# Head 0's row maxima in one part or in two: the start of attention in a two-block graph and attention kernel

## The chip, the cores and the metric

One core of a Trainium2 chip runs the whole program. The metric is device time in microseconds (us), the median of three runs. Before the change it is 898.85 us (897.73 to 899.95).

## The reference

Four blocks act on a matrix `x` of 1354 rows by 256 columns, each with a residual: a graph product with an adjacency matrix, an attention block with a mixture of experts, a graph attention block, and a second mixture of experts. The change touches the attention alone. Cut to what matters it is, with 8 heads of width 32:

```
h = layernorm(x)*g + b
q = h@wq + bq;  k = h@wk + bk;  v = h@wv + bv      # 1354 x 256, 8 heads of 32
scores = q_h @ k_h.T / sqrt(32)                    # 1354 x 1354 per head
attn = softmax(scores, axis=-1)                    # every row minus its own maximum
ctx = attn @ v_h
x = x + ctx @ wo + bo
```

## The kernel before, in words

The 1354 rows are padded to 11 tiles of 128. Every engine has its own instruction list in program order and waits on semaphores: TensorE (PE) multiplies, VectorE (DVE), ScalarE (ACT) and GpSimd (POOL) do elementwise work, SyncE (SP) issues most DMAs. `q` and `k` are each written to memory as a high and a low part, then loaded as "stacks" for one head (`load_stack`, L605): `q_st` and `k_st` have 96 rows of head width (high, high, low against high, low, high), and two more rows in which `q_st` carries the negated row maxima and `k_st` carries ones. So one product gives scores with the maximum already taken off.

**Projections.** `q` and `k` are made in 16 pieces (`qk_product`, L1179). The last 8 belong to heads 4 to 7 and are made while head 0 is already being worked on. For each of these 8, ACT makes two copies (`qk_high`, L897, lines L903 and L904), POOL subtracts (L758), and SP stores the high and the low part (`store_qk`, L589, lines L593 and L595). Three buffers rotate. ACT does not start the first exponential until all stores have landed (L932), because the exponentials' buffers lie over the projections' buffers.

**Maxima.** Row maxima are found in "slots". A slot (`fill_slot`, L1201, on PE; `empty_slot`, L1727, on DVE) is one product of 128 query rows by 452 keys (L1212) and one `tensor_reduce` that takes the maximum of each row (L1736). Three such chunks cover a row tile, 33 a head. The slots share three PSUM banks, so slot i waits until slot i-3 is emptied. When a head's 33 chunks are done, three small DVE instructions make the negated maxima as a high and a low part (`neg_max`, L1740, lines L1743, L1745 and L1747). Later a special slot, the "turn" (list `TURN`, L541), transposes them on PE (L1207), DVE copies them to `m_rows` (L1733), and SP loads that into the two extra rows of `q_st` (`load_max`, L616, line L618). SP issues it for head 0 behind the stores of the projections and ahead of the third stack.

**Scores and values.** With maxima in place, PE computes the scores of a head transposed, in units of 128 keys by 452 queries (`scores`, L1216, line L1224); three thirds of the queries by 11 key tiles make 33 units a head. ACT takes the exponential of each (`exps`, line L915), and PE multiplies it with the values (`values`, L1228, line L1232; two records a unit in the trace, because the operands are full fp32). The units go in groups of 4, 4 and 3 (`GROUPS`). The order on PE is written out by hand (L1263 to L1282): in "phase" j PE alternates a slot and a score unit of group j+1, then fills what slots are left of those allotted to the phase, then does the values of group j. A third's values leave PSUM once per 3 phases (`copy_third`).

**How the slots are spread.** `BESIDE` = 4 slots follow each of the 8 late projection pieces, slots 32 to 41 stand alone (`FILL` = 42), then four score units of group 0, then phase 0 begins. `slots_by(phase)` (L552) gives phases 0 to 13 these numbers of slots: 5, 5, 5, 5, 4, 5, 5, 5, 4, 5, 5, 5, 5, 4. From phase 14 on it is 3 or 4 each. The turns are slots 35, 71, 105 and so on. There are 272 slots, and the last is in phase 56 of 0 to 71. Beside all this POOL splits the weights of the last block (L786 to L796) into high and low parts, from the end of its last subtraction for the projections.

Of the kernel before, what the change touches and what calls it, by code (L numbers as in the profile page):

```python
# [15 lines left out]
P = 128  # L16
# [99 lines left out]
def build_program(nc, a, out):  # L116
    with ExitStack() as ctx:
# [422 lines left out]

        TURN = [(h + 1) * CHUNKS + h + min(4 if h else 2, (H - 1 - h) * CHUNKS) for h in range(H)]  # L541
        SLOTS = H * CHUNKS + H

# [3 lines left out]

        FILL = TURN[0] + 7
        BESIDE = 4
        AHEAD = 14  # L550

        def slots_by(phase):  # L552

            return min(SLOTS, FILL + -(-SLOTS * (phase + 1) // len(GROUPS)) + min(phase + 1, AHEAD))

# [3 lines left out]
        def _(sp):  # L559
# [55 lines left out]

            def load_max(h):  # L616
                sp.wait_ge(s_mx, TURN[h] + 1)
                sp.dma_start(q_st[h % 3].bitcast(F32)[3 * DK:3 * DK + 2, :].rearrange("c (t p) -> c t p", p=P),  # L618
                             m_rows.bitcast(F32)[:, :]).then_inc(s_mload[h % 3], 16)

# [5 lines left out]
            for n in range(HALF, 2 * HALF):  # L626
                store_qk(n)
            load_max(0)
            load_stack(2)
# [12 lines left out]
            for h in range(H):  # L642
                if h >= 1:
                    if h + 2 < H:
                        if h + 2 == H // 2:
                            stored(2 * HALF)
                        sp.wait_ge(s_s2, h * UNITS)
                        load_stack(h + 2)
                    store_third(h - 1, 2)
                    if h + 1 < H:  # L650
                        load_values((h + 1) % 2, h + 1)
                store_third(h, 0)
                if h + 1 < H:
                    load_max(h + 1)
                if h + 1 < H:
                    store_third(h, 1)
# [452 lines left out]
        def _(pe):  # L1109
# [91 lines left out]
            def fill_slot(i):  # L1201
# [3 lines left out]
                if i in TURN:  # L1205
                    pe.wait_ge(s_hl, TURN.index(i) + 1)
                    pe.transpose(ps[0:2 * T, i % 3, 0:P], m_hl.bitcast(F32)[:, :], ident).then_inc(s_s1, 1)  # L1207
                else:
# [7 lines left out]
            def scores(g):  # L1216

                h, m = divmod(g, UNITS)
                third, kt = divmod(m, T)
                if m == 0:  # L1220
                    pe.wait_ge(s_mload[h % 3], h // 3 * 16 + 16)
                if g >= 3:
# [377 lines left out]
        def _(dve):  # L1600
# [126 lines left out]
            def empty_slot(i):  # L1727
                dve.wait_ge(s_s1, i + 1)
                if i in TURN:
                    h = TURN.index(i)  # L1730
                    if h >= 1:
                        dve.wait_ge(s_mload[(h - 1) % 3], (h - 1) // 3 * 16 + 16)
                    dve.tensor_copy(m_rows[:, :], ps[0:2 * T, i % 3, 0:P]).then_inc(s_mx, 1)  # L1733
                else:
                    h, n = chunk_of(i)
                    dve.tensor_reduce(mx4[:, n // KB, n % KB:n % KB + 1], ps[:, i % 3, 0:KC], AX_X, ALU.max).then_inc(s_mx, 1)  # L1736
                    if n == CHUNKS - 1:
                        neg_max(h, i)

            def neg_max(h, i):  # L1740

                dve.wait_ge(s_mx, i + 1)
                dve.tensor_reduce(negm[:, :], mx4[:, :, :], AX_X, ALU.max).then_inc(s_mq, 1)  # L1743
                dve.wait_ge(s_mq, h * 2 + 1)
                dve.tensor_scalar(m_hl[:, 0:T], negm[:, :], -1.0, None, ALU.mult).then_inc(s_mq, 1)  # L1745
                dve.wait_ge(s_mq, h * 2 + 2)
                dve.scalar_tensor_tensor(out=m_hl[:, T:2 * T], in0=negm[:, :], scalar=-1.0, in1=m_hl.bitcast(F32)[:, 0:T],  # L1747
                                         op0=ALU.mult, op1=ALU.subtract).then_inc(s_hl, 1)

# [496 lines left out]
```

## Time and profile before

| | |
|---|---|
| median of three runs | 898.85 us (897.73 to 899.95) |
| profiled execution, own time | 897.19 us |
| its span | 895.4 us |
| granted TensorE clock, mean over the span | 0.928 |
| late projection pieces with slots beside | 98.06 to about 118.5 us |
| first score unit of head 0 | 124.92 us |
| first exponential of head 0 | 125.73 us |
| phases 0 to 13 | 126.87 to 181.11 us |
| last slot | 322 us |
| last value product of head 7 | 367 us |

The profile is one execution. Its span runs from its first to its last instruction, and its own time has 1.8 us more around it. A timeline row gives the start, the length, the engine, the line, what is written and read, and how many instructions were merged; in brackets stands how long the engine sat idle before and what released it. PE instructions overlap, so a start tells more than a length. The PE clock has two levels, 1.0 (2.4 GHz) and 0.5 (1.2 GHz); a value between them is a mean over a stretch that has both.

### The profile page before, as it was taken

The numbers are of one execution on the slowest core, as the hardware profiler recorded it, in microseconds if no ns is written. First come the engines' busy times: TensorE is split into PE (matmuls) and PEld (weight loads), VectorE is DVE, ScalarE is ACT, GpSimd is POOL, SyncE is SP. The second block draws the span as 40 slices with busy tenths as digits, with TensorE's granted clock in tenths as the row PEclk, the third lists the DMA queues.
The fourth block names the chain that finished last, engine by engine and source line by source line (L and its number), as shares of the span: only waits on it lengthen the run. The fifth ranks groups of instructions, "written<-read, shape, count | busy, mean of one in ns | idle before, by whom it ended". The sixth has DMA issues, their size and how long they took to land. (4 is left out here: it accounts for less than half of the span.)

```text
span 895.4 us, 13738 instructions
## 1 busy us (share of the span) xinstructions
PE 781.5 (87%) x4218; PEld 588.8 (66%) x4219; DVE 602.7 (67%) x1164; ACT 410.8 (46%) x840; POOL 315.6 (35%) x322
## 2 busy tenths in 40 slices
PE   3897999999999999843999974999768999999993
PEld 3895655555555543533999972687746888888882
DVE  6575677766666687774989865697593656665661
ACT  3224434556655656351666732631332444445441
POOL 2100246667665766714433004000011343334422
PEclk9998979999999999975999996999758999999997
DMA  7537766887787667633345305950652387752210
GB/s 268 191 95 283 197 205 224 253 264 252 253 267 243 232 200 232 219 112 132 131 147 212 120 26 190 388 187 15 279 182 80 50 269 228 229 154 36 32 17 0
DMA packets 60782, 158.86 MB, mean 177 GB/s; under 512 B 20796, under 2 KB 39034, under 8 KB 57788
## 3 DMA queue, kind: packets, MB, share of 16 engines
q1 hardware_dynamic: 39788, 97.85, 32.2%
q0 software_dynamic: 20944, 60.38, 21.9%
q8 instruction: 27, 0.44, 0.2%
q14 instruction: 23, 0.19, 0.1%
HBM read 103.00 MB, written 49.93 MB: 171 GB/s over the span
## 5 line engine op out<-in xcount | busy, mean ns | idle before, releaser
L1736 DVE TENSOR_REDUCE mx<-ps 128x1 f32<-128x452 f32 x264 | 148.1, 621 | 65.7 <-PE ps L1212 64.8
L915 ACT ACTIVATE expo<-ps 128x452 f32<-128x452 f32 x264 | 124.3, 551 | 92.6 <-PE ps L1224 91.5
L1092 ACT ACTIVATE h<-ps,b_l 128x128 f32<-128x128 f32 x232 | 63.2, 384 | 123.7 <-PE ps L1555 120.2
L1232 PE MATMUL ps<-expo,v_st 128*64 128x452 f32 (+1 forms) x576 | 117.3, 529 | 0.0
L1212 PE MATMUL ps<-k_st,q_st 96*128 96x452 f32 x264 | 106.6, 417 | 4.7 <-DVE mx L1736 4.4
L1224 PE MATMUL ps<-q_st,k_st 98*128 98x452 f32 x264 | 97.1, 392 | 2.0 <-ACT expo L915 2.0
L852 POOL DMA_INDIRECT out<-y1t,out_row x29 | 46.2, 1592 | 124.5 <-DVE share L2129 97.3
L2147 DVE COPY h1pre<-ps 128x1024 f32<-128x1024 f32 x29 | 35.5, 1225 | 78.5 <-PE ps L1548 78.5
L1568 PE MATMUL ps<-w_ring,h_hi 128*128 x232 | 84.2, 400 | 2.8 <-DVE y1t L2156 2.8
L1212 PEld LDWEIGHTS ps<-k_st,q_st 96*128 96x128 f32 x264 | 51.0, 193 | 51.7 <-DVE mx L1736 34.8
L792 POOL TENSOR_TENSOR part_lo<-part,part_hi 128x512 fp32r<-128x512 f32 x64 | 80.9, 1289 | 0.5
L835 POOL DMA_INDIRECT x1t<-x_d,goal x29 | 29.8, 1028 | 135.8 <-DVE goal L2103 115.3
L1232 PEld LDWEIGHTS ps<-expo,v_st 128*64 128x64 f32 x576 | 35.4, 137 | 54.3 <-issue 46.5
L1570 PE MATMUL ps<-w_ring,h_lo 128*128 x232 | 65.7, 283 | 0.0
L1224 PEld LDWEIGHTS ps<-q_st,k_st 98*128 98x128 f32 x264 | 50.3, 195 | 17.8 <-ACT expo L915 9.2
L806 POOL DMA_INDIRECT xs<-x_d,goal x24 | 33.1, 1380 | 69.4 <-PE ps L1350 36.9
L786 POOL CAST part_hi<-part 128x1024 fp32r<-128x1024 f32 x32 | 36.0, 1124 | 55.8 <-DMA part<-w_l 55.8
L1568 PEld LDWEIGHTS ps<-w_ring,h_hi 128*128 128x128 f32 x232 | 44.2, 191 | 13.8 <-issue 3.3
L1546 PE MATMUL ps<-w_ring,x_hi 128*128 x116 | 49.6, 428 | 3.9 <-issue 3.8
L1134 PE MATMUL ps<-hid_hi,adj_hi 128*128 128x256 f32 x121 | 33.0, 303 | 17.6 <-ACT adj_hi L887 17.6
L981 ACT ACTIVATE h<-ps,b_l 128x272 f32<-128x272 f32 x64 | 31.1, 486 | 35.6 <-issue 20.1
L1548 PE MATMUL ps<-w_ring,x_lo 128*128 x116 | 46.7, 403 | 0.0
(322 smaller groups left out, 1792.9 us busy)
## 6 DMA issues: line engine op xcount, KB each, us to landing
w_l<-w_l SPq DMA_DIRECT2D x8, 2053.0 KB, 8.4
part<-w_l POOLq DMA_DIRECT2D x32, 512.0 KB, 5.4
w_split_d<-part_hi POOLq DMA_DIRECT2D x32, 512.0 KB, 3.5
w_split_d<-part_lo POOLq DMA_DIRECT2D x32, 512.0 KB, 3.9
adj<-adj_t SPq DMA_DIRECT2D x22, 704.0 KB, 5.0
w_ring<-w_split_d SPq DMA_DIRECT2D x8, 1365.5 KB
w_ring<-w_split_d SPq DMA_DIRECT2D x4, 1365.0 KB
q_st<-q_hi_d SPq DMA_DIRECT2D x16, 176.0 KB, 3.8
```

Of the source, the lines that this page charges most:

```text
L792: last = pool.tensor_tensor(part_lo[k][:, half], part[k][:, half], part_hi.bitcast(F32)[:, half], ALU.subtract)
L852: pool.indirect_dma_start(out=out[:, :], out_offset=bass.IndirectOffsetOnAxis(ap=out_row[:, t:t + 1], axis=0), in_=y1t[t % 2][:, :], in_of ...
L915: act.activation(expo[g % 8][:, :], ps[:, 3 + g % 3, 0:QC], ACT.Exp, scale=SCALE).then_inc(s_exp, 1)
L1092: last = act.activation(h1[:, f, :], ps[:, 4 + f // 4, (f % 4) * P:(f % 4 + 1) * P], ACT.Gelu_apprx_tanh, bias=b1_l1[:, bass.ds(e, 1), f])
L1212: pe.matmul(ps[:, i % 3, 0:KC], q_st[h % 3][0:3 * DK, (n // KB) * P:(n // KB + 1) * P], k_st[h % 3][0:3 * DK, (n % KB) * KC:(n % KB + 1) * ...
L1224: pe.matmul(ps[:, 3 + g % 3, 0:QC], k_st[h % 3][0:3 * DK + 2, kt * P:(kt + 1) * P], q_st[h % 3][0:3 * DK + 2, third * QC:(third + 1) * QC] ...
L1232: return pe.matmul(ps[at:at + 2 * DK, 6 + g // T % 2, lo:hi], v_st[h % 2][:, kt, :], expo[g % 8][:, lo:hi], start=kt < 2, stop=kt == T - 1 ...
L1546: pe.matmul(ps[:, 2 + b, :], x1_hi[:, kt, :], part_of(at), start=kt == 0, stop=False)
L1548: mm = pe.matmul(ps[:, 2 + b, :], x1_lo[:, kt, :], part_of(at), start=False, stop=kt == DT - 1)
L1568: pe.matmul(ps[:, 6, :], h1_hi[k][:, f, :], part_of(at, 2 * D), start=f == 0, stop=False, skip_group_check=True)
L1570: mm = pe.matmul(ps[:, 6, 0:D], h1_lo[k][:, f, :], part_of(at, D), start=False, stop=f == FT - 1, skip_group_check=True)
L1736: dve.tensor_reduce(mx4[:, n // KB, n % KB:n % KB + 1], ps[:, i % 3, 0:KC], AX_X, ALU.max).then_inc(s_mx, 1)
```

## The change

Head 0's maxima get two turns. The first (slot 14) comes when row tiles 0 to 3 have their maxima, which cover the 452 queries of the first third; the second (slot 36) carries tiles 4 to 10. The first score units of head 0 wait only for the first load, those of the second third wait for the second load. Three slots follow each late projection piece, none stands alone ahead of the scores (`FILL` = 24), and the phases get 7, 7, 7, 7, 6, 7, 7, 7, 7, 6, 6, 4, 4, 4 slots up to phase 13, after which the count is that of before with the one turn more. The other heads keep one turn each, one to two slots later in number. SP issues the first load after the store of the fifth late piece and the second where the only one stood.

```diff
-        TURN = [(h + 1) * CHUNKS + h + min(4 if h else 2, (H - 1 - h) * CHUNKS) for h in range(H)]
-        SLOTS = H * CHUNKS + H
+        EARLY = -(-QC // P)
+        TURN = [EARLY * KB + 2] + [(h + 1) * CHUNKS + h + 1 + min(4 if h else 2, (H - 1 - h) * CHUNKS) for h in range(H)]
+        TURNED = [(0, 0, EARLY), (0, EARLY, T)] + [(h, 0, T) for h in range(1, H)]
+        SLOTS = H * CHUNKS + len(TURN)
...
-        FILL = TURN[0] + 7
-        BESIDE = 4
-        AHEAD = 14
+        def maxima_landed(h):
+            return h // 3 * 16 + (32 if h % 3 == 0 else 16)
+
+        BESIDE = 3
+        FILL = BESIDE * HALF
+        AHEAD = 32
+        CATCH_UP = 3
 
         def slots_by(phase):
 
-            return min(SLOTS, FILL + -(-SLOTS * (phase + 1) // len(GROUPS)) + min(phase + 1, AHEAD))
+            return min(SLOTS, FILL + -(-SLOTS * (phase + 1) // len(GROUPS)) + min(CATCH_UP * (phase + 1), AHEAD))
...
-            def load_max(h):
-                sp.wait_ge(s_mx, TURN[h] + 1)
-                sp.dma_start(q_st[h % 3].bitcast(F32)[3 * DK:3 * DK + 2, :].rearrange("c (t p) -> c t p", p=P),
-                             m_rows.bitcast(F32)[:, :]).then_inc(s_mload[h % 3], 16)
+            def load_max(n):
+                h, lo, hi = TURNED[n]
+                sp.wait_ge(s_mx, TURN[n] + 1)
+                sp.dma_start(q_st[h % 3].bitcast(F32)[3 * DK:3 * DK + 2, lo * P:hi * P].rearrange("c (t p) -> c t p", p=P),
+                             m_rows.bitcast(F32)[0:2 * (hi - lo), :]).then_inc(s_mload[h % 3], 16)
...
             for n in range(HALF, 2 * HALF):
                 store_qk(n)
-            load_max(0)
+                if (n - HALF + 1) * BESIDE == TURN[0] + 1:
+                    load_max(0)
+            load_max(1)
             load_stack(2)
...
                 if h + 1 < H:
-                    load_max(h + 1)
+                    load_max(h + 2)
...
                 if i in TURN:
                     pe.wait_ge(s_hl, TURN.index(i) + 1)
-                    pe.transpose(ps[0:2 * T, i % 3, 0:P], m_hl.bitcast(F32)[:, :], ident).then_inc(s_s1, 1)
+                    h, lo, hi = TURNED[TURN.index(i)]
+                    pe.transpose(ps[0:2 * (hi - lo), i % 3, 0:P], m_hl.bitcast(F32)[:, 2 * lo:2 * hi], ident).then_inc(s_s1, 1)
...
-                if m == 0:
-                    pe.wait_ge(s_mload[h % 3], h // 3 * 16 + 16)
+                if g == 0:
+                    pe.wait_ge(s_mload[0], 16)
+                elif m == (T if h == 0 else 0):
+                    pe.wait_ge(s_mload[h % 3], maxima_landed(h))
...
-                    dve.tensor_copy(m_rows[:, :], ps[0:2 * T, i % 3, 0:P]).then_inc(s_mx, 1)
+                    turn = TURN.index(i)
+                    h, lo, hi = TURNED[turn]
+                    if turn == 1:
+                        dve.wait_ge(s_mload[0], 16)
+                    elif turn:
+                        dve.wait_ge(s_mload[(h - 1) % 3], maxima_landed(h - 1))
+                    dve.tensor_copy(m_rows[0:2 * (hi - lo), :], ps[0:2 * (hi - lo), i % 3, 0:P]).then_inc(s_mx, 1)
...
+                    if (h, 0, n // KB + 1) in TURNED[:1] and n % KB == KB - 1:
+                        neg_max(0, i)
                     if n == CHUNKS - 1:
-                        neg_max(h, i)
-
-            def neg_max(h, i):
-
+                        neg_max(h + 1, i)
+
+            def neg_max(turn, i):
+
+                _, lo, hi = TURNED[turn]
                 dve.wait_ge(s_mx, i + 1)
-                dve.tensor_reduce(negm[:, :], mx4[:, :, :], AX_X, ALU.max).then_inc(s_mq, 1)
+                dve.tensor_reduce(negm[:, lo:hi], mx4[:, lo:hi, :], AX_X, ALU.max).then_inc(s_mq, 1)
...
```

The two other instructions of `neg_max` are cut to the same tiles in the same way.

## Rows read from the trace of the kernel before

**Rows 1.** The page's costliest group: busy, mean ns, idle before it.
```profile
L1736 DVE TENSOR_REDUCE mx<-ps 128x1 f32<-128x452 f32 x264 | 148.1, 621 | 65.7 <-PE ps L1212 64.8
```
**Rows 2.** Timeline of PE, late projections to first scores: start, length, instruction, idle before.
```profile
99.08 1.05 PE L1212 MATMUL ps<-k_st,q_st 96*128 96x452 f32 x3
100.44 0.47 PE L1212 MATMUL ps<-k_st,q_st 96*128 96x452 f32 x1 [0.31 <-DVE mx L1736]
100.75 1.35 PE L1185 MATMUL ps<-nt,w_attn 128*128 128x352 f32 x4
...
116.26 1.35 PE L1185 MATMUL ps<-nt,w_attn 128*128 128x352 f32 x4
...
124.92 2.15 PE L1224 MATMUL ps<-q_st,k_st 98*128 98x452 f32 x4
```
**Rows 3.** Timeline of DVE, head 0's negated maxima.
```profile
120.65 0.19 DVE L1743 TENSOR_REDUCE negm<-mx 128x11 f32<-128x33 f32 x1
...
121.17 1.16 DVE L1736 TENSOR_REDUCE mx<-ps 128x1 f32<-128x452 f32 x2
...
122.24 0.27 DVE L1733 CAST m_rows<-ps 22x128 fp32r<-22x128 f32 x1
```
**Rows 4.** Timeline of all engines: last projection piece from copy to store, first exponential.
```profile
117.64 0.51 ACT L903 ACTIVATE proj<-ps,vecs 128x298 f32<-128x298 f32 x1 [1.59 <-PE ps L1185]
...
119.02 0.93 POOL L758 TENSOR_TENSOR proj_lo<-proj,proj_hi 128x352 fp32r<-128x352 f32 x1 [1.96 <-ACT proj_hi L904]
...
119.98 0.32 SPq L595 DMA_DIRECT2D k_lo_d<-proj_lo  x1
...
125.73 1.93 ACT L915 ACTIVATE expo<-ps 128x452 f32<-128x452 f32 x4 [6.79 <-PE ps L1224]
```
**Rows 5.** DMA issues by tensor: KB each, median us from issue to landing.
```profile
k_lo_d<-proj_lo SPq DMA_DIRECT2D x8, 176.0 KB, 1.8
```
**Rows 6.** Stretches by engine: us, busy (count) of PE, PEld, DVE, ACT, POOL; PE clock; DMA.
```profile
121.00:122.00 1.00, 0.53 (x2) 0.25 (x2) 0.97 (x4) 0.00 (x0) 0.00 (x0) 0.67 0.90 184
131.00:132.00 1.00, 1.00 (x6) 0.38 (x4) 0.13 (x1) 0.00 (x0) 0.00 (x0) 0.71 0.99 397
```
**Rows 7.** The same columns for phases 0 to 13 together, 1, 4, 5 and 12.
```profile
126.87:181.11 54.24, 52.28 (x231) 28.73 (x229) 39.11 (x73) 27.11 (x57) 35.31 (x39) 0.96 0.76 244
132.63:136.42 3.79, 3.77 (x18) 1.91 (x16) 2.77 (x5) 1.43 (x3) 3.48 (x5) 1.00 0.47 156
143.64:146.96 3.32, 3.32 (x17) 1.73 (x16) 2.23 (x4) 1.42 (x3) 2.44 (x3) 1.00 0.89 263
146.96:151.89 4.93, 3.62 (x19) 2.08 (x17) 4.17 (x8) 1.86 (x4) 3.24 (x4) 1.00 0.52 188
173.40:178.00 4.60, 4.01 (x19) 2.10 (x17) 3.47 (x8) 2.41 (x5) 3.62 (x5) 1.00 0.71 247
```
**Rows 8.** Timeline of PE inside phases 0 and 3.
```profile
130.39 2.31 PE L1232 MATMUL ps<-expo,v_st 128*64 128x452 f32 x8
...
139.84 0.47 PE L1212 MATMUL ps<-k_st,q_st 96*128 96x452 f32 x1
...
141.64 0.40 PE L1212 MATMUL ps<-k_st,q_st 96*128 96x452 f32 x1
141.97 1.74 PE L1232 MATMUL ps<-expo,v_st 128*64 128x452 f32 x8
```
**Rows 9.** Timeline of all engines in phase 5, with head 1's negated maxima.
```profile
147.47 0.63 DVE L1736 TENSOR_REDUCE mx<-ps 128x1 f32<-128x452 f32 x1 [1.09 <-PE ps L1212]
...
148.34 1.03 POOL L786 CAST part_hi<-part 128x1024 fp32r<-128x1024 f32 x1 [1.96 <-DMA part<-w_l]
...
148.36 1.04 DVE L1745 TENSOR_SCALAR m_hl<-negm 128x11 fp32r<-128x11 f32 x1
...
149.52 2.23 DVE L1736 TENSOR_REDUCE mx<-ps 128x1 f32<-128x452 f32 x4
150.20 0.19 PEld L1212 LDWEIGHTS ps<-k_st,q_st 96*128 96x128 f32 x1 [1.70 <-DVE mx L1736]
```

More of the change, by code:

```diff
@@ L1729, in empty_slot @@
                 if i in TURN:
-                    h = TURN.index(i)
-                    if h >= 1:
-                        dve.wait_ge(s_mload[(h - 1) % 3], (h - 1) // 3 * 16 + 16)
-                    dve.tensor_copy(m_rows[:, :], ps[0:2 * T, i % 3, 0:P]).then_inc(s_mx, 1)
+                    turn = TURN.index(i)
[5 more added lines that the diff above has]
+                    dve.tensor_copy(m_rows[0:2 * (hi - lo), :], ps[0:2 * (hi - lo), i % 3, 0:P]).then_inc(s_mx, 1)
                 else:
@@ L1736, in empty_slot @@
                     dve.tensor_reduce(mx4[:, n // KB, n % KB:n % KB + 1], ps[:, i % 3, 0:KC], AX_X, ALU.max).then_inc(s_mx, 1)
+                    if (h, 0, n // KB + 1) in TURNED[:1] and n % KB == KB - 1:
+                        neg_max(0, i)
                     if n == CHUNKS - 1:
-                        neg_max(h, i)
-            def neg_max(h, i):
+                        neg_max(h + 1, i)
+            def neg_max(turn, i):
+                _, lo, hi = TURNED[turn]
                 dve.wait_ge(s_mx, i + 1)
-                dve.tensor_reduce(negm[:, :], mx4[:, :, :], AX_X, ALU.max).then_inc(s_mq, 1)
[L1744 to L1748, printed above, removed]
+                dve.tensor_reduce(negm[:, lo:hi], mx4[:, lo:hi, :], AX_X, ALU.max).then_inc(s_mq, 1)
+                dve.wait_ge(s_mq, turn * 2 + 1)
+                high, low = slice(2 * lo, lo + hi), slice(lo + hi, 2 * hi)
+                dve.tensor_scalar(m_hl[:, high], negm[:, lo:hi], -1.0, None, ALU.mult).then_inc(s_mq, 1)
+                dve.wait_ge(s_mq, turn * 2 + 2)
+                dve.scalar_tensor_tensor(out=m_hl[:, low], in0=negm[:, lo:hi], scalar=-1.0,
+                                         in1=m_hl.bitcast(F32)[:, high], op0=ALU.mult, op1=ALU.subtract).then_inc(s_hl, 1)
             def normalize(c, cols, placed, rows_at=slice(0, P)):
```

## The prediction

> **What bounds the kernel now.** I read the page first: in a span of 895.4 us the costliest group is the maxima's reduce, 264 times 0.62 us [rows 1]. Then the timelines of PE, DVE and ACT around the start of attention, and last the stretches of single phases.
>
> Three regimes follow each other. Beside the late projections PE and DVE alternate: a fourth slot waits 0.31 us for a bank, and the piece behind it starts 0.31 us after that slot [rows 2]; the pieces start 2.585 us apart ((116.26 - 100.75)/6). Then ten slots run alone until the first scores at 124.92. Here DVE is the bound, at 0.54 us a slot ((2.23 - 0.62)/3 [rows 1, 9]), and PE does so little that its clock falls to half within the second from 121 and comes back in the second from 131 [rows 6]. From 126.87 on come the phases. There PE is the bound: over phases 0 to 13 it is busy 52.28 of 54.24 us, DVE 39.11 [rows 7]. A phase with 5 slots takes 3.79 us, one with 4 takes 3.32. So everything up to the last value product is a serial stretch set by PE's program order, and what starts earlier in it is won only if the phases do not grow by as much.
>
> **What is won ahead of phase 0.** With three slots a piece, the bank wait goes. Three slot products span 1.05 us from 99.08; with equal steps of a third the last starts at about 99.76 (an estimate). The next piece starts 0.31 us behind the last slot, so each piece comes 100.44 - 99.76 = 0.68 us sooner after its predecessor: 2.585 - 0.68 = 1.90 us. DVE needs 3 x 0.54 = 1.6 us and fits. The last piece then starts at 116.26 - 7 x 0.68 = 111.5 us, 4.8 us earlier. Head 0's first negated maxima (three DVE steps, 121.17 - 120.65 = 0.5 us [rows 3]) fall in DVE's slack of 0.3 us a piece and cost PE nothing or 0.2; without that slack they would cost 0.5. The first load stands in SP's list behind the fifth piece's stores; it delays the next store by under 0.8 us, and three buffers cover that.
>
> The ten lone slots go too, but ACT cannot start when PE reaches the scores (about 113): it waits for the last store. Now: copy at 117.64, subtraction until 119.95, store issued 119.98, 1.8 us to land [rows 4, 5], so 121.8; the first exponential comes only at 125.73 because the slots and the load stand ahead. After: 121.8 - 4.8 = 117.0 us. Bounds: 116.5 (pieces 0.06 us faster each) and 117.8 (a late landing of 2.6 us). So the first exponential comes 8.7 us earlier, and PE sits mostly idle from 113 to 117. That idle stretch is what remains of the gain: 12 us of slots removed, 8.7 realised. Phase 0 begins 126.87 - 125.73 = 1.14 us behind, at 118.1.
>
> **The clock in phase 0.** PE's clock fell after the thin stretch of 118.5 to 121 and came back 6.7 us after the scores began. The new stop of 4 us is thinner still, so I take half clock again, for the same 6.7 us from the third score unit's release at 117.5, to about 124.2. At half clock now values of phase 0 start 3.52 us after its first slot (130.39 - 126.87) against 2.13 at full clock (141.97 - 139.84) [rows 8]. Two more slots at 0.38 each: 4.3 us, at 122.4. Their 1.67 us (143.64 - 141.97) begin at half rate, 1.8 us of it, and end at 124.9. Phase 1 therefore starts at 124.9 where it now starts at 132.63: 7.7 us earlier. Bounds: 123.6 if the clock is back one step sooner, 126.5 if one later.
>
> **What the phases pay.** At full clock a phase runs so: slots and scores alternate, the fifth slot starts at +1.80 (141.64 - 139.84) and the values 0.33 behind it [rows 8]. Slot i+3 may start 0.68 us after slot i's reduce starts (150.20 - 149.52 [rows 9]), the first reduce starts at +0.51 (147.47 - 146.96), the others 0.54 apart. The sixth slot waits for the third reduce: 0.51 + 2 x 0.54 + 0.68 = 2.27; the seventh: 2.81. Values follow a waited slot by 0.40. So the values start at 2.13 with five slots, at 2.67 with six, at 3.21 with seven: each further slot costs 0.54 us, DVE's price, where PE's own work on it is 0.2. With four slots it is 1.65 (3.32 - 1.67).
>
> Against before, phases 1 to 13: six of them go from 5 to 7 slots, 6 x 1.08 = 6.5; phase 4 from 4 to 6, 1.0; phase 8 from 4 to 7, 1.4 (one score more than in phase 4 stands ahead of its values, 0.2 us of the 1.6); phases 9 and 10 from 5 to 6, 1.1; phases 11 and 12 from 5 to 4, between -0.3 and -0.5 each, -0.7. Sum 9.3 us. A turn's copy takes 0.27 instead of 0.54 and there is one more: -0.3.
>
> The second part of head 0's negated maxima now comes in phase 1, in the bound path of DVE. Its cost lies between 0.6 (beside the projections now) and 1.5 us: in phase 5 the same three steps reach from 148.1 to 149.52, one of them 1.04 us long from 148.36 on, as POOL's cast runs from 148.34 [rows 9], and that phase takes 4.93 us where one with five slots and three units of values takes 139.84 - 136.42 = 3.42. I take 1.1. Heads 1 and 2 pay such stalls before (4.93 - 3.42 = 1.5 us, and in phase 12 4.60 - 3.79 = 0.8 us [rows 7]); after the change head 1's steps stand in the middle of phase 6, head 2's at the end of phase 11 with the values ahead of the next slot: -0.9 for both, between -2.3 and 0.
> The Trainium skill (GPSIMD Engine Reference, Specifications) says that GpSimd shares its SBUF interfaces with VectorE and contends with DVE instructions in a 2-port mode or with two SBUF inputs. By that rule the new place is worse than the old one, since POOL is idle at 120.7 and splits weights throughout the phases; taken whole it would give 1.5 instead of 1.1, and the sum 0.4 us more.
>
> The second load: the copy of slot 36 ends about 4.2 us into phase 1, the first score unit that waits for it comes behind the rest of the slots, 1.67 us of values and one slot, at about 6.1. Now at most 2.4 us lie between the copy's end (122.51) and the first score unit (124.92) [rows 2, 3], and 1.8 us is what a 16 times larger store takes. So the wait is 0 to 0.5 us; I take 0.3. Behind it on PE everything queues. The third stack's load moves behind this second load on SP, from 123.4 to about 130 us, and is first needed by slot 68, in phase 6 (about 150): nothing.
>
> Sum for phases 1 to 13: 9.3 - 0.3 + 1.1 - 0.9 + 0.3 = 9.5 us, between 8 and 12. From phase 14 on both kernels have the same slots per phase, and POOL's split starts 4.8 us earlier, so it delays nothing.
>
> **Total:** -7.7 + 9.5 = +1.8 us. Made against the profiled execution (897.19 us) that is 899.0; it lies 1.7 us under the median, so for the median 898.85 + 1.8 = 900.7 us.
>
> **The rivals.**
> *B, the slots hide.* The 19 added slots cost PE's price, 19 x 0.21 = 4 us, instead of 9.3: -3.5 us, 895.4. For it: DVE is idle 28% of the phases [rows 7]. Against: three banks tie each slot to the reduce three before, and the fifth slot alone costs 0.47 us already.
> *C, the clock stays down (slower).* The idle PE of 113 to 117 and then slots that wait in each phase keep it at half clock beyond phase 0. A phase of seven slots at half clock takes 4.3 us to its values and 3.3 for them, 7.6 us instead of 4.9, so 2.7 us a phase. It decides from the first such phase: +4.5 us with one, 903.4; +7.2 with two, 906. For it: at half clock before, 6.7 us of work passed before it came back. Against: full-clock phases with a wait of 1.7 us [rows 9] kept it.
> *D, no fall at all.* Phase 0 takes 4.9 us instead of 6.8, the sum is 0, 898.8 us.
> *E, the change does nothing:* excluded, since the order on PE is written out.
>
> **Chances.** Forecast 0.55 (own range 898.5 to 903), B 0.10, C 0.22, D 0.13. No change means within 0.3%, 2.7 us, about what a measurement can tell. The forecast's upper part (0.13) lies beyond it, and C. Faster 0.10 (B), same 0.55 (0.42 and D), slower 0.35. The range for 8 in 10 takes in the forecast, D and C with one phase, and stops short of B: 897 to 904.5.
>
> **What would show it.** Late pieces 1.9 us apart. First exponential near 117, ACT released by nothing on PE. PE idle for 3 to 4 us before it, granted clock 0.5 in phase 0 and 1.0 from about 124. Seven-slot phases 4.8 to 4.9 us long with two waits for L1736 in each, four-slot phases unchanged. Phase 14 starts near 183, not 181.1. I am wrong if seven-slot phases take under 4.3 us (B), if half clock reaches phase 2 (C), if pieces are 2.3 us apart or more (the stores' three buffers bind), or if the exponentials wait for a landing after 118.

## The result, and the profile after

The kernel after took 908.32 us (median of 4 executions) beside 899.4 us for the kernel before on the same chip, a ratio of 1.0108 (95% interval 1.0065 to 1.0152). A repeat with twelve executions gave 909.9 beside 900.85 us, ratio 1.0073 (1.0036 to 1.0109). The ratio is smaller than that of the two medians, which lie 9.05 us apart; both are given where they differ. The change makes the kernel 3 to 14 us slower; the forecast was +1.8 us, its range ended at 904.5. The first profile of the kernel after is of its slowest execution (920.1 us), so what follows is read from the repeat's, with a span of 911.0 us and 912.81 us for its own time. That is 15.6 us above the profiled execution of before, so it shows more than the typical loss, and the sizes below are checked against medians.

The page's groups of the maxima's reduce and of the slot products, kernel after (busy, mean ns, idle before); the first answers to [rows 1].

```profile
L1751 DVE TENSOR_REDUCE mx<-ps 128x1 f32<-128x452 f32 x264 | 148.4, 621 | 68.1 <-PE ps L1222 66.0
...
L1222 PE MATMUL ps<-k_st,q_st 96*128 96x452 f32 x264 | 106.2, 415 | 4.2 <-DVE mx L1751 3.0
```

The reduce still costs 621 ns, and the page puts only 3.0 us of PE's idle time down to it (4.4 in before): the loss is not in stops for slots. Next the timeline of PE alone, kernel after, from the late pieces to the values of phase 2 (start, length, instruction, idle before and its releaser); the late pieces are now L1194, slots L1222, scores L1236, values L1244.

```profile
100.28 1.35 PE L1194 MATMUL ps<-nt,w_attn 128*128 128x352 f32 x4
...
102.14 1.35 PE L1194 MATMUL ps<-nt,w_attn 128*128 128x352 f32 x4
...
108.69 0.27 PE L1217 MATMUL ps<-const,m_hl 128*8 128x128 f32 x1 [1.14 <-DVE m_hl L1766]
...
112.46 1.35 PE L1194 MATMUL ps<-nt,w_attn 128*128 128x352 f32 x4
...
118.66 0.75 PE L1236 MATMUL ps<-q_st,k_st 98*128 98x452 f32 x1 [2.57 <-ACT expo L924]
...
123.48 2.11 PE L1244 MATMUL ps<-expo,v_st 128*64 128x452 f32 x8
125.52 0.47 PE L1222 MATMUL ps<-k_st,q_st 96*128 96x452 f32 x1
...
128.51 0.27 PE L1217 MATMUL ps<-const,m_hl 128*14 128x128 f32 x1 [0.79 <-DVE m_hl L1766]
...
131.03 0.47 PE L1222 MATMUL ps<-k_st,q_st 96*128 96x452 f32 x1
135.83 0.74 PE L1236 MATMUL ps<-q_st,k_st 98*128 98x452 f32 x1 [4.33 <-DMA q_st<-m_rows]
...
139.89 2.06 PE L1244 MATMUL ps<-expo,v_st 128*64 128x452 f32 x8
141.88 0.47 PE L1222 MATMUL ps<-k_st,q_st 96*128 96x452 f32 x1
...
146.75 0.47 PE L1222 MATMUL ps<-k_st,q_st 96*128 96x452 f32 x1
```

Up to 131 us this is the forecast's course: pieces about 1.85 us apart (but 3.00 where the first turn is waited for), an idle stretch before the first exponentials, phase 1 from 125.52 instead of 132.63. Then PE stands 4.33 us for head 0's second load. All engines around it, kernel after (POOL's split is now L795 to L805, the load's issue L625; SPq is SyncE's queue, its length is that of the issue):

```profile
128.43 0.54 POOL L797 DMA_DIRECT2D w_split_d<-part_hi  x1 [0.30 <-POOL part_hi L795]
...
129.09 0.53 POOL L775 DMA_DIRECT2D part<-w_l  x1
129.35 0.27 DVE L1748 CAST m_rows<-ps 14x128 fp32r<-14x128 f32 x1
129.36 1.74 PE L1244 MATMUL ps<-expo,v_st 128*64 128x452 f32 x8
...
129.65 0.68 SPq L625 DMA_DIRECT2D q_st<-m_rows  x1
130.37 0.87 SPq L614 DMA_DIRECT2D q_st<-q_hi_d  x2
```

The copy ends at 129.62, the load is issued at 129.65 and PE goes on at 135.83: 6.2 us for 7 KB. Ahead of it POOL issued two transfers of 512 KB each, at 128.43 and 129.09; the third stack's loads follow it on SP from 130.37. The stretches in which this falls, kernel after, with the columns of [rows 6] (phase 0, phase 1, behind the load's issue, the stop, phase 2, phase 3):

```profile
119.00:121.00 2.00, 2.00 (x6) 1.78 (x6) 1.05 (x2) 1.59 (x5) 0.61 (x1) 0.50 0.29 119
126.00:127.00 1.00, 1.00 (x6) 0.78 (x5) 0.97 (x2) 0.76 (x2) 0.23 (x1) 1.00 0.51 201
...
129.60:131.00 1.40, 1.40 (x8) 0.29 (x4) 0.56 (x2) 0.00 (x0) 1.38 (x3) 1.00 0.89 351
...
134.00:135.00 1.00, 0.00 (x0) 0.00 (x0) 0.00 (x0) 0.00 (x0) 0.00 (x0) 0.76 0.87 160
...
136.00:140.00 4.00, 4.00 (x12) 3.04 (x14) 2.64 (x5) 2.19 (x4) 1.81 (x2) 0.50 0.97 321
142.00:143.50 1.50, 1.50 (x8) 1.29 (x8) 1.11 (x3) 1.45 (x4) 1.50 (x2) 1.00 0.79 262
```

The clock is half in phase 0, as forecast, and full in phase 1. Behind the load's issue the DMA engines are busy 0.89 of the time at 351 GB/s. In the stop PE, DVE and ACT stand still and the clock falls, and phase 2 runs at half.

Where the time went is read best from the start of each phase's value products (rows "PE ... expo,v_st ... x8" of each kernel's timeline), in us after the kernel before's own (130.39, 134.76, 138.55, 145.29, 182.95, 238.43, 364.54):

| phase | 0 | 1 | 2 | 4 | 14 | 31 | 70 |
|---|---|---|---|---|---|---|---|
| after (the repeat) | -6.9 | -5.4 | +1.3 | +4.1 | +8.2 | +12.1 | +10.9 |
| after_hold | -8.5 | -7.4 | -6.0 | -3.9 | +1.1 | +4.5 | +4.7 |
| turns_only | -3.0 | -3.2 | -3.2 | -3.3 | -4.7 | -1.0 | -0.3 |
| before_nosplit | +1.9 | +2.3 | +2.3 | +2.3 | +1.2 | +1.2 | -0.2 |
| after_nosplit | -8.4 | -7.0 | -1.6 | +1.8 | +5.0 | +5.0 | +4.6 |
| nosplit_hold | -9.4 | -6.4 | -3.8 | -1.7 | +1.5 | +1.4 | -0.3 |
| fill32 | -1.2 | +0.1 | +0.7 | +1.7 | +7.0 | +6.9 | +8.6 |

Each row is one execution against one. That of the kernel before took 897.19 us, and its medians beside the experiments are 3.7 to 6.0 us above that, so the differences to it in the table look larger than they typically are.

### The profile page after: what moved, and what is told of

Its sections match the earlier page's. It is cut to its first block and busy times, and to the rows that moved or that the text cites. A ratio compares the mean times of both kernels' runs of the same rounds, so it can differ in the third digit from the quotient of the medians.

```text
span 918.3 us, 13748 instructions
## 1 busy us (share of the span) xinstructions
PE 792.5 (86%) x4219; PEld 595.2 (65%) x4220; DVE 613.3 (67%) x1168; ACT 411.7 (45%) x840; POOL 314.5 (34%) x322
## 5 line engine op out<-in xcount | busy, mean ns | idle before, releaser
L1244 PE MATMUL ps<-expo,v_st 128*64 128x452 f32 (+1 forms) x576 | 120.6, 541 | 0.0
L1222 PE MATMUL ps<-k_st,q_st 96*128 96x452 f32 x264 | 106.9, 417 | 6.3 <-DVE mx L1751 4.8
L1236 PE MATMUL ps<-q_st,k_st 98*128 98x452 f32 x264 | 99.3, 398 | 9.2 <-ACT expo L924 4.6
L1222 PEld LDWEIGHTS ps<-k_st,q_st 96*128 96x128 f32 x264 | 51.8, 197 | 50.4 <-DVE mx L1751 34.3
L1244 PEld LDWEIGHTS ps<-expo,v_st 128*64 128x64 f32 x576 | 36.0, 140 | 56.5 <-issue 47.8
L1236 PEld LDWEIGHTS ps<-q_st,k_st 98*128 98x128 f32 x264 | 51.1, 198 | 26.2 <-ACT expo L924 11.6
L1558 PE MATMUL ps<-w_ring,x_hi 128*128 x116 | 50.5, 435 | 4.0 <-issue 3.8
L795 POOL CAST part_hi<-part 128x1024 fp32r<-128x1024 f32 x32 | 35.3, 1102 | 51.4 <-DMA part<-w_l 51.4
L1559 PE MATMUL ps<-w_ring,x_hi 128*128 x116 | 47.1, 406 | 0.0
```

The lines of the kernel that those rows point to most:

```text
L1222: pe.matmul(ps[:, i % 3, 0:KC], q_st[h % 3][0:3 * DK, (n // KB) * P:(n // KB + 1) * P], k_st[h % 3][0:3 * DK, (n % KB) * KC:(n % KB + 1) * ...
L1236: pe.matmul(ps[:, 3 + g % 3, 0:QC], k_st[h % 3][0:3 * DK + 2, kt * P:(kt + 1) * P], q_st[h % 3][0:3 * DK + 2, third * QC:(third + 1) * QC] ...
L1244: return pe.matmul(ps[at:at + 2 * DK, 6 + g // T % 2, lo:hi], v_st[h % 2][:, kt, :], expo[g % 8][:, lo:hi], start=kt < 2, stop=kt == T - 1 ...
L1558: pe.matmul(ps[:, 2 + b, :], x1_hi[:, kt, :], part_of(at), start=kt == 0, stop=False)
L1559: pe.matmul(ps[:, 2 + b, :], x1_hi[:, kt, :], part_of(LO1 + at), start=False, stop=False)
```

## The experiments

Each was timed beside the kernel before on the same chip, in 12 executions (nosplit_hold in 8, nosplit_fill32 in 6). Ratios are to the kernel before, with the 95% interval; medians in us, and beside them the median of the kernel before that goes with them.

| kernel | median | before | ratio |
|---|---|---|---|
| after_again | 909.9 | 900.85 | 1.0073 (1.0036 to 1.0109) |
| after_hold | 904.62 | 900.85 | 1.0031 (0.9999 to 1.0063) |
| turns_only | 901.16 | 900.85 | 0.9999 (0.9966 to 1.0033) |
| four_beside | 902.54 | 900.85 | 1.0029 (0.9997 to 1.0060) |
| before_nosplit | 897.04 | 900.91 | 0.9957 (0.9929 to 0.9984) |
| after_nosplit | 899.86 | 900.91 | 0.9986 (0.9961 to 1.0012) |
| nosplit_hold | 896.92 | 902.14 | 0.9939 (0.9905 to 0.9973) |
| nosplit_fill32 | 895.38 | 902.14 | 0.9904 (0.9867 to 0.9942) |
| before_lean | 905.32 | 900.91 | 1.0043 (1.0015 to 1.0072) |
| hold_lean | 905.66 | 900.91 | 1.0049 (1.0022 to 1.0077) |
| fill32 | 903.03 | 903.22 | 0.9993 (0.9960 to 1.0026) |
| fill32_hold | 902.61 | 903.22 | 0.9992 (0.9963 to 1.0021) |

**after_again** is the kernel after unchanged.

> The changed kernel once more, for its profile and a narrower interval. Theory W (the second load is late): value products of group 1 start near 129.8 us, PE then stops about 3.5 us for the load of head 0's second maxima, issued at about 130.1 and landing 5.4 us later, and phase 2 runs at half clock; total 907 to 909 us. Theory L (the stalls are an alignment of DVE's small steps with POOL's split): the stop for the load is under 1 us in this execution, and the loss sits in stalls of 2 to 4 us at turns of later heads. The stalls at later turns should come at other heads than in the first profile under both, since POOL's split is not tied to the slots.

The loss came again, and with it the wait: in the profile first taken it was 3.54 us, here 4.33 us. The stalls at later turns moved in part only: head 2's came again, at 212 us, others did not.

**after_hold**: POOL keeps its second part's transfers back until the second load has landed.

```
+                if n == 1:
+                    pool.wait_ge(s_mload[0], 32)
                 pool.dma_start(split_rows(n, 0), shaped(n, part_hi.bitcast(F32))).then_inc(s_hi_out, 16)
```

> The changed kernel, with one more wait on POOL: it does not store the high half of its second weight part until head 0's second load has landed. So no transfer of POOL runs beside that load, except what was issued before. Theory W, with the load slowed by POOL's transfers of 512 KB: the load lands 2 to 2.5 us after its issue, the stop on PE shrinks from 3.5 us to under 0.7, the clock stays up in phase 2, and the total is 5 to 6 us lower than the changed kernel, 902 to 904. Rival W2 (the load is slow in itself, since it is many small rows behind one issue): it still lands after 4.5 to 5.5 us, total unchanged, 907 to 909. Rival L: total within 1.5 us of the changed kernel.

All engines, after_hold, from the load's issue to the values of phase 2 (its lines are two further down):

```profile
127.67 0.68 SPq L625 DMA_DIRECT2D q_st<-m_rows  x1
...
129.66 0.47 PE L1238 MATMUL ps<-q_st,k_st 98*128 98x452 f32 x1
...
130.15 0.54 POOL L799 DMA_DIRECT2D w_split_d<-part_hi  x1 [2.74 <-DMA q_st<-m_rows]
...
132.54 1.36 PE L1246 MATMUL ps<-expo,v_st 128*64 128x452 f32 x8
```

And its stretches from issue to landing, and of phase 2:

```profile
127.60:129.70 2.10, 1.96 (x10) 0.51 (x6) 0.72 (x3) 0.00 (x0) 0.00 (x0) 1.00 0.18 41
...
130.00:132.00 2.00, 1.99 (x9) 1.30 (x7) 1.81 (x5) 1.83 (x4) 1.83 (x3) 1.00 1.07 256
```

The same load, with the same stack loads behind it on SP, meets DMA engines that are busy 0.18 of the time and lets PE go on 2.0 us after its issue; the stop is gone and phase 2 runs at full clock. From the values of phase 1 to those of phase 4 it takes 13.96 us instead of 20.06, 6.1 us less; by phase 14, 5.2 us of this are left. The median fell by 5.3 us (by the ratios, 3.8 of 6.6; the two intervals overlap). So POOL's transfers are what delays the load, and by the medians and the traces the delay is most of the loss.

**turns_only** and **four_beside** keep the two turns of head 0, but four slots a piece, with the lone slots of before or without them.

```
-        BESIDE = 3
-        FILL = BESIDE * HALF
-        AHEAD = 32
-        CATCH_UP = 3
+        BESIDE = 4
+        FILL = 42              # four_beside: BESIDE * HALF
+        AHEAD = 14             # 20
+        CATCH_UP = 1           # 2
...
-                if (n - HALF + 1) * BESIDE == TURN[0] + 1:
+                if n - HALF == TURN[0] // BESIDE:
```

> One part of the change alone: head 0's maxima in two turns, but the schedule of before (four slots beside each piece, 42 slots ahead of the scores, the same slots a phase with the one turn more). Theory W: the extra turn costs 0.3 to 0.8 us and the second load lands ahead of its need, so 899 to 901 us, no different from before. Rival T (the second turn or the narrower loads cost something by themselves): 903 or more.

> The two turns with another schedule: four slots beside each late projection piece as before the change, 32 ahead of the first scores, then 6, 6, 6, 6, 5, 6, 6, 6, 6, 5 slots a phase (CATCH_UP 2, AHEAD 20, FILL 32). Slot 36 now lies in phase 0, so the second load has a whole phase of lead. Theory W with the DVE price for each slot: first exponential near 121.9 us, no stop for the second load, 10 slots moved into the phases of which about 6 are paid at 0.54 us; total 898 to 901 us. Rival S (three slots beside are what saves time, and moving slots into phases costs nothing but the load's wait): total higher than a changed kernel without the load's wait, above 903.

Two turns alone cost nothing that can be measured. In the profile of turns_only the value products of phases 14 and 20 start 4.7 us earlier than in before, those of phase 22 only 0.9 us and those of phase 70 only 0.3 us earlier. The lead goes at head 2's maxima, where a DVE step of 0.17 us lasts 2.72 us. All engines, turns_only:

```profile
199.17 2.72 DVE L1764 TENSOR_SCALAR m_hl<-negm 128x11 fp32r<-128x11 f32 x1
...
199.31 2.53 POOL L801 TENSOR_TENSOR part_lo<-part,part_hi 128x512 fp32r<-128x512 f32 x2
```

four_beside, expected at 898 to 901 us, took 902.54 and lies between. Its profile is 0.6 us behind before at phase 4 and 7.0 at phase 8; in between DVE's TENSOR_SCALAR for head 1's maxima lasts 2.80 us instead of 0.17, and PE waits 3.08 us for the slot behind it. The kernel after has the same thing. All engines, kernel after, head 2's maxima:

```profile
212.06 0.17 DVE L1764 TENSOR_SCALAR m_hl<-negm 128x11 fp32r<-128x11 f32 x1
...
212.26 2.96 DVE L1766 SCALAR_TENSOR_TENSOR m_hl<-negm,m_hl 128x11 fp32r<-128x11 f32 x1
...
212.67 2.52 POOL L801 TENSOR_TENSOR part_lo<-part,part_hi 128x512 fp32r<-128x512 f32 x2
...
215.81 0.47 PE L1222 MATMUL ps<-k_st,q_st 96*128 96x452 f32 x1 [2.10 <-DVE mx L1751]
```

The step ends as POOL's two subtractions do, though by the trace it had begun 0.41 us before them. From phase 20 to 22 the value products fall back by 4.1 us there, and that is all that the kernel after loses between phases 14 and 31.

**before_nosplit** and **after_nosplit** take the split's arithmetic on POOL out of either kernel and leave its transfers. POOL's subtractions for the projections stay. The transfers of a part now wait for eight more exponentials, so they lie at other times than with the split, and a gain could in part be theirs.

```
-                pool.tensor_copy(part_hi[:, :], part[k][:, :]).then_inc(s_part_split, 1)
-                pool.wait_ge(s_part_split, 2 * n + 1)
-                pool.dma_start(split_rows(n, 0), shaped(n, part_hi.bitcast(F32))).then_inc(s_hi_out, 16)
+                pool.wait_ge(s_exp, PRIMED + 8 * n)
+                pool.dma_start(split_rows(n, 0), shaped(n, part[k])).then_inc(s_hi_out, 16)
...
-                for half in (slice(0, SPLIT // 2), slice(SPLIT // 2, SPLIT)):
-                    last = pool.tensor_tensor(...)
-                last.then_inc(s_part_split, 1)
-                pool.wait_ge(s_part_split, 2 * n + 2)
-                pool.dma_start(split_rows(n, 1), shaped(n, part_lo[k].bitcast(F32))).then_inc(s_lo_out[k], 16)
+                pool.dma_start(split_rows(n, 1), shaped(n, part[k])).then_inc(s_lo_out[k], 16)
```

> The kernel before, with POOL's computing left out: its casts and subtractions of the last block's weights are gone (the stored halves are plain copies of the weights, so the last block's values are not the reference's), and its transfers are paced by the exponentials, one weight part per eight of them. Theory L (DVE's small steps are held while POOL computes): no L1745 or L1747 step longer than 0.3 us, the stalls of 1.5 and 0.8 us at the turns of heads 1 and 2 shrink to 0.3 at most, and the value products end 2 to 5 us sooner, total 895 to 898. Rival (the long steps have another cause): steps up to 1 us or more stay.

> The changed kernel with the same part of POOL left out and its transfers paced the same way. Together with the kernel before in this form it gives the price of the schedule with neither the held DVE steps nor POOL's transfers beside the second load. Theory W (late load) and D (each slot moved into the phases costs DVE's 0.54 us): the load lands within 2.5 us, value products of group 14 start 0.5 to 2.5 us later than in the kernel before in this form, and the difference stays the same to the end of attention. Rival (the price of the moved slots is larger than 0.54 us each): a difference over 4 us.

DVE's two steps on m_hl, by tile, first of the kernel after, then of after_nosplit (least, median and longest ns):

```profile
L1764 DVE TENSOR_SCALAR m_hl<-negm x9: 169/172/833, 107.5 to 333.1; 128x11 fp32r<-128x11 f32 x7, 128x4 fp32r<-128x4 f32 x1, 128x7 fp32r<-128x7 f32 x1
L1766 DVE SCALAR_TENSOR_TENSOR m_hl<-negm,m_hl x9: 168/171/2959, 107.7 to 333.8; 128x11 fp32r<-128x11 f32 x7, 128x4 fp32r<-128x4 f32 x1, 128x7 fp32r<-128x7 f32 x1
```

```profile
L1758 DVE TENSOR_SCALAR m_hl<-negm x9: 170/172/175, 106.7 to 326.1; 128x11 fp32r<-128x11 f32 x7, 128x4 fp32r<-128x4 f32 x1, 128x7 fp32r<-128x7 f32 x1
L1760 DVE SCALAR_TENSOR_TENSOR m_hl<-negm,m_hl x9: 161/171/172, 106.9 to 326.3; 128x11 fp32r<-128x11 f32 x7, 128x4 fp32r<-128x4 f32 x1, 128x7 fp32r<-128x7 f32 x1
```

Without the split's arithmetic no step is held in these two, and the phases from 14 to 31 take what they take in before: +5.0 and +5.0 us in the table. Both kernels gain, the one before 0.4%, the one after 0.9%. The rest of what was expected did not come: before_nosplit's last value products start 0.2 us earlier than before's, not 2 to 5, and those of phase 14 in after_nosplit 3.8 us after before_nosplit's, not 0.5 to 2.5. And the stop for the load stays:

```profile
128.10 0.68 SPq L625 DMA_DIRECT2D q_st<-m_rows  x1
...
132.91 0.75 PE L1230 MATMUL ps<-q_st,k_st 98*128 98x452 f32 x1 [2.97 <-DMA q_st<-m_rows]
```

(all engines, after_nosplit). Ahead of this load POOL had issued three transfers of 512 KB, 2.4, 1.2 and 0.7 us before. So the late load needs POOL's transfers, not its arithmetic, and what remains between the two kernels is 2.8 us.

**nosplit_hold** is after_nosplit with the two lines of after_hold, to price the late load where no held step stirs the time.

> The kernel after without POOL's casts and subtractions (its copies of each part are stored twice, so the last block's values are not the reference's, as before), and POOL does not issue the second part's stores and next load before head 0's second load has landed. Without that hold the same kernel took 2.8 us more than the kernel before without POOL's arithmetic, and PE stood 2.97 us for the load, landing 4.8 us after its issue, with phase 2 at half clock behind it. Theory (the late load is the cost, the slots' price the small rest): load lands 2.0 to 2.4 us after its issue, no stop, the values of group 2 start at about 132.5 instead of 136.98 us, those of group 14 at about 184, and the median is 3 to 5 us lower, 895 to 897. Rival (the slots and the clock fall of phase 0 are the cost, the stop only takes a wait that comes anyway): group 14 within 1 us of 188.0, the median at 899 to 900. Rival (the landing is slow by itself behind the stack loads on SP): it still lands after 4 us or more and nothing changes.

It took 0.9939 of before, after_nosplit 0.9986: the late load costs 4.2 us by the ratios, whose intervals overlap, and 2.9 by the medians. And nosplit_hold is as fast as before_nosplit (0.9957): with the load in time and no step of the phases held, the change costs nothing that can be measured, and the slots' price is paid by the earlier start: at phase 14 its values start 0.3 us after before_nosplit's. The load, issued at 128.55, had landed by 131.43, when POOL, which waits for it, issued its store: 2.9 us at most. The values of phase 2 started later than expected, at 134.77. The clock was full again from 125 on and then fell once more inside phase 1 (nosplit_hold, the columns of [rows 6]), behind a turn and not behind a load:

```profile
125.00:126.00 1.00, 1.00 (x6) 0.72 (x4) 1.00 (x2) 0.84 (x2) 0.00 (x0) 1.00 0.04 16
...
129.00:130.00 1.00, 1.00 (x6) 0.32 (x4) 0.09 (x1) 0.00 (x0) 0.00 (x0) 0.50 0.02 5
```

So phase 1's values took 3.3 us instead of 1.7, and part of the wait would have been hidden under them in any case.

**before_lean** and **hold_lean** put fewer slots ahead, so that the last phases have fewer; the first is the kernel before, the second after_hold.

```
-        AHEAD = 14             # hold_lean: AHEAD = 32
+        AHEAD = 6              # 24
```

> The kernel before with AHEAD 6 instead of 14: eight slots fewer in phases 5 to 13, the last slot in phase 59 instead of 56. Same reasoning as for the changed schedule: group 14's values about 3.5 us sooner (the fifth slot of a phase costs 0.47 us), the last about 1.5 to 2 us sooner, total 897 to 900. Rival (slots cost the same wherever they stand): no difference from the kernel before.

> The changed kernel with POOL's transfers held for the second load, and AHEAD 24 instead of 32: phases 8 to 10 get 4, 3 and 4 slots instead of 7, 6 and 6, and the last slot comes in phase 59 instead of 56. By the price of 0.54 us for a slot beyond the fourth in a phase and some 0.2 to 0.3 for one in the phases behind the last slot, the value products of group 14 start about 4 us earlier than with the hold alone and those of group 63 about 2 us earlier: total 900 to 902. Rival (slots cost the same wherever they stand): no difference from the hold alone. Rival (the maxima come too late for some head): stops on L1236 for a load.

Both forecasts failed: hold_lean is no faster than after_hold, and before_lean is slower than before, by 1.4 to 6.5 us. In before_lean's profile the last value products start 6.1 us earlier than in before, at 358.43, and nothing comes of it. PE alone, before_lean, behind the last values:

```profile
367.29 3.35 PE L1256 MATMUL ps<-ctx_raw,head_sums 128*128 128x452 f32 x4 [2.65 <-DVE nt L1766]
```

DVE's chain behind its last maxima is what ends late; in hold_lean PE waits the same 2.65 us for it. It begins with the copy of the last maxima and runs through the normalisations to the nt that PE waits for. DVE alone, kernel before, its start and its longest wait:

```profile
322.58 3.07 DVE L1772 TENSOR_TENSOR u_or_h<-u_or_h,rows 128x2816 f32<-128x2816 f32 x1
...
359.10 1.10 DVE L1755 TENSOR_TENSOR den_even<-den_even,den_odd 128x452 f32<-128x452 f32 x1 [3.67 <-DMA den_odd<-ctx_raw]
```

DVE alone, kernel after, the same start, and PE alone behind it:

```profile
334.66 3.07 DVE L1791 TENSOR_TENSOR u_or_h<-u_or_h,rows 128x2816 f32<-128x2816 f32 x1
...
381.36 0.63 DVE L1785 TENSOR_TENSOR nt<-ps,den_even 32x452 f32<-32x452 f32 x1
```

```profile
382.14 1.75 PE L1268 MATMUL ps<-ctx_raw,head_sums 128*128 128x452 f32 x4 [2.65 <-DVE nt L1785]
```

In before the chain has about 6 us of waits for ctx_raw in it, so both bounds end almost together; in the kernel after it has none left up to 382 us (two steps on nt take 3.14 and 3.43 us there, for 0.63 in before), and PE waits for it: its last sums start 13.8 us after before's, its last values 10.9. So the end of attention has two bounds: PE's last values, and DVE's last maxima plus 42 to 48 us (from their copy at 324.84 to 367.29 in before_lean, from 334.45 to 382.14 in the kernel after). Where the second ends last, to move PE alone gains nothing. In before_lean the last maxima are copied 2.5 us later than in before. That this makes the 4 us of its ratio is not shown: its profile, at 898.55 us, is of the fastest of its twelve executions.

**fill32** and **fill32_hold**: eight slots more ahead of the first scores, in PE's idle stretch; the second with the hold.

```
-        FILL = BESIDE * HALF
-        AHEAD = 32
-        CATCH_UP = 3
+        FILL = BESIDE * HALF + 8
+        AHEAD = 24
+        CATCH_UP = 2
...
-                if (n - HALF + 1) * BESIDE == TURN[0] + 1:
+                if n - HALF == TURN[0] // BESIDE:
```

> The two turns, three slots beside each late piece, but eight more slots in the stretch in which PE waits for the last store (FILL 32), then CATCH_UP 2 and AHEAD 24: 6, 6, 6, 6, 5, 6, 6, 6, 6, 5, 6, 6 slots a phase, and the same count as both kernels from phase 12 on. Theory (late second load, DVE's price for slots in the phases, and DVE's work after the last slot as the second bound at the end of attention): slot 36 lies in phase 0 and the load has over 5 us of lead, so PE does not stop for it; first exponential near 120.4 us, group 14's values 0 to 2 us sooner than in the kernel before, last slot 0 to 2 us sooner, total 897 to 901. Rival (idle PE ahead of the exponentials is not where the loss was): group 14's values 2 us or more behind the kernel before, total above 903.

> The same with POOL's transfers held until the second load has landed. If that load has enough lead anyway, as the theory says, the hold brings nothing: total within 1.5 us of the run without it. Rival (the hold helps for another reason than the load's wait, such as the third stack's load or POOL's alignment): 3 us or more below it.

Both take the time of before, 0.9993 and 0.9992. The load is issued while nothing waits for it (PE's waits list none for it in fill32), and the hold adds nothing there: its gain in after_hold is not the hold's own. The forecast of the course missed: the first exponential comes at 122.34 us (120.4 expected), and the values of phase 14 start 7.0 us after before's instead of 0 to 2 us ahead, in an execution of 906.05 us. In fill32's profile three of DVE's steps on m_hl take 2.3 to 2.5 us, one of them at head 0's second turn, in fill32_hold's four take 2.5 to 2.8.

**nosplit_fill32** is fill32 without the split's arithmetic, by the edit of after_nosplit.

> The kernel after without POOL's casts and subtractions (last block's values not the reference's), with 32 slots ahead of the first scores instead of 24, so that PE has slots in its idle time before the first exponentials. With POOL's arithmetic this order took the time of the kernel before (903.03 beside 903.22 us) though its value products ended 8.6 us later than in one execution of it. Theory (once DVE's steps are not held, the order itself costs what the slots cost at DVE's price, nearly paid by the earlier start): within 1.5 us of the kernel before without POOL's arithmetic, whose ratio was 0.9957, so 0.994 to 0.998 of the kernel before. Rival (DVE's work at the end is the bound and comes later by the phases' growth): 1.000 or more, as the kernel after without POOL's arithmetic, 0.9986, or above.

0.9904 of the kernel before, the fastest kernel run, below the expected 0.994. Its values of phase 2 start 6.6 us and those of phase 14 4.1 us before those of the kernel before. No kernel with POOL's split in it beat the kernel before. Of the gain here, 0.4% is that of before_nosplit, which has the old order; the rest, some 5 us by the ratios, would be the order's, but the intervals of the two ratios overlap, so it is likely and not shown. Where else the split could go was not tried.

## Why the prediction was wrong

*Right.* The pieces came about 1.85 us apart (1.90 forecast), but for the one behind the first turn. The first exponential came at 118.06 us (ACT, row not shown; forecast 117.0): the last store was issued 1.0 us later than forecast, at 116.19, and landed in 1.87 us. The microsecond is the wait of 1.14 us for the turn, which I had put at 0 to 0.2: beside POOL's subtraction of a late piece the last of the three steps took 0.87 us instead of 0.17. In after_hold it was not held, the wait was 0.43 us, and the first exponential came at 117.07. PE idled before the exponentials, the clock was half in phase 0, and its values started at 123.48 (122.4). Phase 1 started 7.1 us earlier (7.7). The copy of the second maxima ended 4.1 us into phase 1 and the first score unit was due at about 6.0 (4.2 and 6.1). The phases' arithmetic held as well: phase 3, with seven slots, took 4.87 us (141.88 to 146.75; 4.8 to 4.9 forecast). The rival in which slots hide is refuted: in after_hold, with the load in time, the lead of 7.4 us at phase 1's values was gone by phase 14. There phase 14's values started 1.1 us after before's where the sum said 1.8, and that nearness is in part luck: phase 1 began 9.1 us earlier, not 7.7, and phases 1 to 13 grew by 10.3 us, not by the 9.2 that the sum has without its wait (phase 12 alone took 5.32 us there, with a held step in it, and 3.50 in the kernel after). The 1.1 us charged for the second part's three steps in phase 1 were too much for this execution: they took 0.17 to 0.19 us each, the first two of them beside POOL's cast, which ran until 128.14. In fill32 one of them took 2.31 us.

*The step that failed* is the second load: "the wait is 0 to 0.5 us; I take 0.3". It was 4.33 us, and behind it the clock fell again; together 6.1 us by phase 4, and 2.9 to 5.3 us of the time by the two pairs of kernels with and without the hold. The bounds came from rows of another place: head 0's load in before, which has one 512 KB load of POOL's ahead of it, issued 2.5 us earlier, and the k_lo_d stores at 1.8 us [rows 3, 5]. The new place is inside the phases, where POOL's split stores and loads 512 KB at a time, here 1.2 and 0.6 us ahead. I had POOL's cast in [rows 9] and used it for DVE's price alone. With the transfers held back the load took 2.0 us, inside the 1.8 to 2.4 us that I had; the step that failed is that I took a price from a place without that traffic.
The Trainium skill (DMA: Bandwidth & Descriptors, Anatomy of one DMA — SWDGE (gpsimd) path) gives a transfer on POOL's queue a fixed cost of about 2.0 us, beside the time of its bytes; this load on SP's queue took as much in after_hold, 2.0 us, and the 6.2 us under POOL's transfers are beyond that rule.

*The rival C* had the half clock in a later phase, at 2.7 us for one seven-slot phase, and that did occur, in phase 2. But I had it as phase 0's clock that never comes back. In fact the clock was full in phase 1 and fell after a new stop. Phase 2 at half clock cost only about 1.1 us beyond the stop, and phase 3 another 0.7.

*"From phase 14 on ... it delays nothing"* was a second miss, of a smaller size. DVE's short steps are held while POOL computes: 2.96 us for 0.17 here, against at most 1.04 in the profile of before. The forecast charged this once, 1.1 us for the first heads, and took no chance of it for the others. Where a step meets POOL differs from execution to execution: the first profile of the kernel after has four steps of 1.6 to 2.8 us, the repeat's only this one above 1 us. The spread of the times fits that (the kernel after between 901.85 and 917.66 us in the repeat, without the split's arithmetic between 897.99 and 904.65). So this is partly noise of both kernels; that the change makes it more frequent is not shown.
The Trainium skill (SBUF — State Buffer, Who interferes with whom) says that a DVE step with two inputs in SBUF contends with a GpSimd step that reads SBUF, and that of a DVE step in a 2-port mode and a GpSimd step the one issued first has the shared ports for its whole instruction while the other is blocked. before_nosplit and after_nosplit agree, all steps at 0.16 to 0.18 us, and so do nosplit_hold and nosplit_fill32, where the one long step (0.92 and 0.84 us) stands beside a projection's subtraction. But the 2.96 us reach over two of POOL's subtractions, not one, and by the trace the DVE step began first.

*Not in the prediction at all:* the end of attention. I let a delay at phase 14 pass to the end one for one. A gain does not pass so: before_lean and hold_lean show that DVE's chain then ends last. A delay does pass, and in the profiled execution of the kernel after DVE's chain, with its two long steps on nt, added 2.9 us to it.

*Left open:* which of POOL's two transfers, the store or the load of a part, is the one that delays the second load; how the remaining +2.8 us of after_hold (0 to 5.7) divides between slots and held steps; and why before_lean's median is above before's.

## What to carry to other kernels

A small transfer's landing time belongs to the place where it is issued: before moving one, look at what every other queue has in flight there, and take its price from a row under the same traffic. A wait on PE is to be priced with the clock behind it. Where two chains end together, as PE's values and DVE's normalisations here, an earlier end of one can be worth nothing, and both must be followed to their common end before a gain is booked.

## What the hardware showed unexpectedly

A load of 7 KB took 6.2 us from issue to its waiter with two 512 KB transfers of another queue ahead of it, 4.8 us in after_nosplit with three ahead, and 2.0 us in after_hold with them behind it. A stop of 4.33 us at full clock was followed by a granted clock of 0.50, although PE had run at 1.00 until then. A DVE step of 128 x 11 elements, 0.17 us alone, took 2.96 us beside two subtractions of POOL.
